# Accumulating transposes for the state-space sums, a reordered Silu, and residuals behind a block border

## The reference

```
x = x + attention(norm(x))      # gated delta rule, 32 value heads of 128
x = x + ffn(norm(x))            # 4-bit weights, 512 -> 1408 -> 512, then y / rms(y)
x = x + state_space(norm(x))    # 512 channels, 16 states
x = x + ffn(norm(x))            # the same weights again
```

```
h[n] = exp(dt * A[n]) * h[n] + dt * x * B[n]
y    = sum over n of h[n] * C[n]          # out = y @ W_out + b
```

## Time and profile before

| | us |
|---|---|
| median of 3 runs | 4491.68 (4491.48 to 4496.43) |
| profiled execution | 4493.62 |
| its span | 4491.8 |
| PE busy | 4303.1 (96%) |
| DVE busy | 3417.9 (76%) |
| ACT busy | 2310.3 (51%) |
| mean granted TensorE clock | 0.986 |

### The profile page before, as it was taken

One profiled execution on the slowest core, in us unless ns is written; L12 is line 12 of the kernel. 1 busy time (PEld: TensorE's weight loads), 2 busy tenths in 40 slices (PEclk: granted clock), 3 DMA queues, 4 the chain that ended last, 5 costly groups with the idle time before them and its releaser, 6 DMA issues. The chain is left out here.

```text
span 4491.8 us, 79320 instructions
## 1 busy us (share of the span) xinstructions
PE 4303.1 (96%) x29557; PEld 2595.2 (58%) x29557; DVE 3417.9 (76%) x8579; ACT 2310.3 (51%) x4841; POOL 433.2 (10%) x342
## 2 busy tenths in 40 slices
PE   7899999999999999999999999998699999999898
PEld 4566666666666666666666666666344444444343
DVE  5888887888877788788788787785446889888950
ACT  4555555555555555555555555554245545554532
POOL 1111111111111111111111111110000000000000
PEclk9999999999999999999999999999899999999999
DMA  2111111101110111110110110100203444444520
GB/s 72 40 37 36 34 36 32 36 32 34 41 32 29 36 36 62 46 32 29 37 36 29 41 32 30 36 29 11 88 1 116 140 134 152 144 154 135 173 73 19
DMA packets 202401, 263.27 MB, mean 59 GB/s; under 512 B 18174, under 2 KB 101378, under 8 KB 202018
## 3 DMA queue, kind: packets, MB, share of 16 engines
q1 hardware_dynamic: 202018, 258.20, 17.9%
HBM read 249.24 MB, written 8.91 MB: 57 GB/s over the span
## 5 line engine op out<-in xcount | busy, mean ns | idle before, releaser
L455 PE MATMUL bank<-xnT,w_qkv 128*128 128x512 f32 x2048 | 928.6, 596 | 4.1 <-ACT raw L741 3.4
L455 PEld LDWEIGHTS bank<-xnT,w_qkv 128*128 128x128 f32 x2048 | 374.7, 192 | 404.6 <-issue 385.9
L1026 DVE SCALAR_TENSOR_TENSOR conv<-raw,conv_w,conv 128x1024 f32<-128x1024 f32 x384 | 495.3, 1290 | 142.4 <-ACT conv L715 133.2
L568 PE MATMUL bank<-w_out_unit,oT 128*128 128x512 f32 x1024 | 504.7, 616 | 7.9 <-ACT oT L781 7.9
L529 PE MATMUL bank<-w_z_unit,xnT 128*128 128x256 f32 x2048 | 487.5, 381 | 0.0
L529 PEld LDWEIGHTS bank<-w_z_unit,xnT 128*128 128x128 f32 x2048 | 371.5, 191 | 41.4 <-issue 1.0
L1237 PE MATMUL bank<-xnT_f,w_gu 128*128 128x512 f32 x704 | 327.6, 609 | 11.1 <-PEq L1560 7.0
L812 ACT ACTIVATE squares<-o 128x128 f32<-128x128 f32 x512 | 153.9, 302 | 336.8 <-DVE o L1070 275.6
L1255 PE MATMUL bank<-w_down,hidden 128*128 128x512 f32 x704 | 316.8, 593 | 1.1 <-DVE x_blocks L1297 1.1
L1245 PE MATMUL bank<-xnT_f,w_gu 128*128 128x512 f32 x704 | 316.5, 592 | 0.0
L655 ACT ACTIVATE q_state<-bank,e_gc 128x128 f32<-128x128 f32 x448 | 140.3, 364 | 263.6 <-PE bank L440 254.8
(11 more groups left out here) (224 smaller groups left out, 7983.6 us busy)
## 6 DMA issues: line engine op xcount, KB each, us to landing
rows_b<-bc_rows SPq DMA_DIRECT2D x256, 256.0 KB, 3.3
rows_c<-bc_rows SPq DMA_DIRECT2D x256, 256.0 KB, 3.4
w_qkv<-in_w_qkv SPq DMA_DIRECT2D x128, 256.0 KB, 2.9
decay<-gc_rows SPq DMA_DIRECT2D x64, 512.0 KB, 3.9
w_z_unit<-in_w_z SPq DMA_DIRECT2D x32, 512.0 KB, 4.4
w_out_unit<-in_w_out SPq DMA_DIRECT2D x32, 512.0 KB, 5.0
x_after<-x SPq DMA_DIRECT2D x16, 256.0 KB, 2.0
x_blocks<-x_after SPq DMA_DIRECT2D x4, 1024.0 KB, 13.2
```

The lines of the kernel that those rows point to most:

```text
L455: made = e.matmul(PROJ[:, :], w_qkv[:, p % 2, j, :], xnT[:, n // HK, j, h * BANK:(h + 1) * BANK], start=j == 0, stop=j == KT - 1)
L568: made = e.matmul(OB[:, :], oT[:, r, :], w_out[:, N % 2, r, :], start=r == 0, stop=r == REP - 1)
L1026: e.scalar_tensor_tensor(acc, raw[:, i % 2, tap:tap + T], conv_w[:, tap, col:col + 1], acc, ALU.mult, ALU.add).then_inc(on["conv"], 1)
```

## The change

There are three edits. In the attention ACT copies raw and u first and applies z's Silu after them; where a unit's z is due, the load of the Exp table follows z's Silu instead of standing before the copies.

In the state space the identity matmul is replaced by four transposes of the pair's sum, 128x128 each, that accumulate in YB, so that YB holds y as [position, channel]. ACT copies it to a new buffer `y_rows`, PE turns that back by channel tile (a new use `y_turn` of the bank WB, at place 0 of the slot 19 after the tile's first step), and ACT copies it to y. Of the out matmuls of stages 0 to 2 the first moves from slot +3 to +4 of the next stage; those of the last stage move from the end of slot +2 to the head of slot +4. Run 7 starts a slot later.

The squares and the residual of run 0 are left out of its block and stand at the head of the next block's ACT and DVE programs.

```diff
-                    if n_z is not None:
-                        N = n_z
-                        e.wait_ge(on["z_evict"], 4 * N + 4)
-                        e.activation(z[:, :, :, :], z[:, :, :, :], ACT.Silu).then_inc(on["z_silu"], 1)
-                    e.preload_act_table_set(EXP_SET)
+                    if n_z is None:
+                        e.preload_act_table_set(EXP_SET)
...
                     e.wait_ge(on["u_pe"], 8 * (n_scan) + t_scan + 1)
                     e.copy(u[:, :, :], two(UB, 0)).then_inc(on["u_copy"], 1)
+
+                if n_z is not None:
+                    e.wait_ge(on["z_evict"], 4 * n_z + 4)
+                    e.activation(z[:, :, :, :], z[:, :, :, :], ACT.Silu).then_inc(on["z_silu"], 1)
+                    e.preload_act_table_set(EXP_SET)
...
-RUN_START = {1: 0, 2: 44, 3: 88, 4: 132, 5: 176, 6: 228, 7: 273}
+RUN_START = {1: 0, 2: 44, 3: 88, 4: 132, 5: 176, 6: 228, 7: 274}
...
+        uses += [(at + 16 * i + 19, 0, ("y_turn", q, i)) for i in range(KT)]
...
-            uses += [(stage_start(q + 1) + (3, 6, 7, 8)[t], 1, ("out", q, t)) for t in range(TILES)]
+            uses += [(stage_start(q + 1) + (4, 6, 7, 8)[t], 1, ("out", q, t)) for t in range(TILES)]
         else:
-            uses += [(stage_start(q + 1) + 2, 1, ("out", q, t)) for t in range(TILES)]
+            uses += [(stage_start(q + 1) + 4, 0, ("out", q, t)) for t in range(TILES)]
...
-                square_down(e, 0)
...
-                add_residual(e, 0)
...
+                elif kind == "y_turn":
+                    e.wait_ge(on["y_copy"], KT * q + i + 1)
+                    made = turn(e, WB, y_rows[:, :])
                 else:
-                    e.wait_ge(on["y_copy"], KT * (q + 1))
+                    e.wait_ge(on["work_read"], WORK_INDEX[("y_turn", q, KT - 1)] + 1)
...
-                    e.matmul(YB[:, :], c["ident"][:, :], drive[:, p % 4, :], start=n == 1, stop=n == NS - 1).then_inc(
-                        on["y_sum"], 1)
+                    for t in range(TILES):
+                        cols = slice(t * P, (t + 1) * P)
+                        made = e.matmul(YB[:, cols], drive[:, p % 4, cols], c["ident"][:, :], start=n == 1 and t == 0,
+                                        stop=n == NS - 1 and t == TILES - 1, is_transpose=True, skip_group_check=True)
+                    made.then_inc(on["y_sum"], 1)
...
+                elif kind == "y_turn":
+                    if i == 0 and q > 0:
+                        e.wait_ge(on["work_made"], WORK_INDEX[("out", q - 1, TILES - 1)] + 1)
+                    e.copy(y[:, i, :], WB[:, :]).then_inc(on["work_read"], 1)
...
+            square_down(e, 0)
             ss_rstd(0)
...
-                    if i == 0 and q > 0:
-                        e.wait_ge(on["work_made"], WORK_INDEX[("out", q - 1, TILES - 1)] + 1)
-                    e.copy(y[:, i, :], YB[:, :]).then_inc(on["y_copy"], 1)
+                    if KT * q + i > 0:
+                        e.wait_ge(on["work_made"], WORK_INDEX[("y_turn", *divmod(KT * q + i - 1, KT))] + 1)
+                    e.copy(y_rows[:, :], YB[:, :]).then_inc(on["y_copy"], 1)
...
+            add_residual(e, 0)
             ss_stats(0)
```

More of the change, by code:

```diff
@@ L1574, in second_half @@
         carry = sb("carry", [P, NS, KT])
-        y = sb("y", [P, KT, BANK])
+        y, y_rows = sb("y", [P, KT, BANK]), sb("y_rows", [P, BANK])
         gate_slot = {at + 4 * i: (R, i) for R, at in RUN_START.items() for i in range(IT)}
```

## The result

The changed kernel takes 4427.71 us (median of four runs, 4426.6 to 4429.21); the kernel before, run beside it, 4494.06 (4491.48 to 4496.78). The ratio is 0.9853, 95% interval 0.9835 to 0.987: 66 us less. The profiled execution of the changed kernel took 4427.73 us, span 4426.0, where the span of before was 4491.8.

What follows compares the result with a forecast made beforehand. PE was taken as the bound, 96% busy, with DVE close behind in the state space; 32.8 + 29 + 1 - 1 = 61.8 us less gave 4430 against the median (chance 0.54), range 4413 to 4448.

Steps and rivals of the forecast that it cites:

- Part 1: Attention: z's Silu behind u's copy on ACT removes PE's whole wait at L552, 31 x 1.06 = 32.8 us; bounds 16, 33.
- Part 2: State space: y sums by transposes take net 46.7 us off PE, of which 29 us come through; bounds 11, 44.
- D: State-space y sums don't run at the short rate, two records a transpose: 20 us lost, 33 gained, 4479; chance 0.04.
- E: State-space y sums: a transpose takes its full 0.273 us; 50 us lost, 33 gained, 4508; chance 0.04.
- The factors three quarters and a half: State space: share of 11.7 us a stage coming through, 8.8 each in stages 0 to 2, 5.9 in stage 3.
- The 2.7 us for a turn behind a turn: State space: four y_turns directly behind a turn ACT must copy out wait 0.68 us each, 2.7 us.
- Rival B: State space: DVE takes over, carry and decay behind y_turn copies; 17 us cost, sums give 12, 4447; chance 0.20.
- Rival C: State space: PE decides throughout, the sums give 44 us, 4415; chance 0.13.
- Rival F: Attention: half of the gain from z's Silu behind u's copy comes back at L568, 4446; chance 0.05.
- Part 3: Border before the state space: run 0's residuals moved; first turn's copy 2.7 us sooner, bc loses 1.7: 1 us gained.
- Part 4: The end, last y sum to out matmuls: y_turn and the wait for y's copy lengthen it, -1 us (0 to -1.5).

Runs made afterwards that it cites:

- run 0: Not a follow-up experiment: a numbered run of work inside the kernel itself, whose squares and residual stood at the end of the preparing block before the change; no time of its own.
- the ordinary matmuls: The changed kernel with the y sums as ordinary f32 matmuls of 128x128 in place of transposes, y_turns still transposes: 4464.06 us, ratio 0.9936 to the kernel before.
- the early Silu: The changed kernel with the Silu of run 1's first gate ahead of the state space's first rstd on ACT: 4432.02 us, ratio 0.9864 to the kernel before.
- part 1 alone: The kernel before with only the attention's order on ACT changed, raw's and u's copies ahead of z's Silu: 4454.86 us, ratio 0.9914.
- part 3 alone: The kernel before with only the squares and residual of run 0 moved into the next block: 4493.0 us, ratio 0.9998.
- parts 2 and 4 alone: The changed kernel with ACT's order in the attention and the border put back as before: 4473.27 us, ratio 0.9955 to the kernel before.
- early Silu with run 6 earlier: The changed kernel with run 1's first Silu ahead of the first rstd and run 6 at slot 224 for 228: 4431.61 us, ratio 0.986 to before.

## Why the prediction was right

It said 4430 and faster; 4427.7 was measured. In the profiled executions, 61.8 less was forecast and 65.9 found (4493.6 and 4427.7). The closeness is in part luck: part 1 was priced 5 us too low and part 2 about 2 too high. By its own steps:

**Part 1, mechanism right, its term 5 us too small.** Forecast 32.8, the upper end of its bounds 33; the attention alone gained 38.0 (start of the last z Silu, 3157.6 to 3119.6). What follows is not late, as argued: PE is without idle time there. But oT's copy is out only 0.15 us before L568 starts, where the prediction's times leave 0.39. Mis-sized was the price of one wait. The profile counts idle time from the modelled end of the instruction ahead, and that end lies late: in the changed kernel L320 is shown until 1474.65, and L552 behind it starts at 1474.49. Taken from start to start it is different. The instruction ahead of L552, in before:

```profile
1490.34 1.13 PE L320 MATMUL bank<-kq 128*128 128x256 f32 x4
```

To L552 at 1492.52 it is 2.18 us; in the changed kernel 0.97 (1473.52 to 1474.49): 1.21 us where the bracket said 1.05. Another 0.11 went behind L552 (L556 came 0.55 us later, now 0.44), most likely the weight load that had nothing to hide behind. That makes 1.32 a unit, close to what the distance of two z Silus shows (95.81 less 94.50). The second slip is the count: the sum took all 31 waits, and two stay, so 29 x 1.32 = 38.3 us, and 38.0 were measured.

**Part 2, size right (27.3 for 29), the share that comes through guessed.** The work came off as computed, 45.2 us for 46.7, 0.44 us for a sum (rivals D and E fell on the first row; the ordinary matmuls show what D would have been, 4464). The 275 ns of the Trainium skill ("TensorE: Matmul & The Clock Gate", Part 4: PE-mode transpose) is not a pitch here: the changed kernel's transposes have 0.109 us each in a group of four.
- The prediction gave two reasons for the share. The first, waits for DVE that a faster PE only reaches sooner, is what the rows show: PE's idle time grew from 28.6 to 43.6 us, nearly all of it beside a busy DVE. The waits that grew, 3.9 us for xn_f, 3.8 for drive, 1.7 for xn_ss and 1.2 for ACT's xnT_f in front of turns, 10.6 of these 15 us, stand where runs and stages meet: normed rows by DVE, a turn, ACT's copy, the next turn. The second, that the two engines are tied step by step so that DVE's idle time can't be moved about, shows only as PE's few waits for drive (four, 10.2 us, for three, 6.4). DVE's total load is not what sets the share: with some 49 us less on it the growth of PE's gaps is the same, 17.8 for 17.9 us. Whether less work of DVE at those borders would let more through stays open.
- The factors three quarters and a half had no measurement behind them. By stage the forecast gains were 8.2, 8.1, 8.1 and 5.9 us, and 6.3, 9.0, 5.1 and 6.9 came. In sum 32.2 of 46.7 was taken as coming through, seven tenths, and 27.3 of 45.2 did, six tenths.
- The 2.7 us for a turn behind a turn: at run 2's turns the wait costs nothing, the hole is there without it. At the three places beside the state space's turns it is real, 1.33, 0.51 and 1.34 us with the turn's own 0.44. How much of that reaches the end is hidden by the clock in the run without turns back.
- By stage 214.5, 228.7, 224.1, 211.9 was forecast, and it became 216.4, 227.8, 227.1 and 210.9. The two that are off by 1.9 and 3.0 us lie under the 4.5 by which the same first stage differs between the full change and the early Silu, so no stage can be called right or wrong.

Rival B (carry behind the copies of turns back) had 0.20 and is refuted: DVE's wait for the carry went from 41.8 to 38.1 us, and taking all turns back out gave 1.3, some 5 at an equal clock. Its sign, stages 0 and 2 unchanged, came in part: they gained least, 6.3 and 5.1. But without turns back these two stages take 219.0 and 226.4 us for 216.4 and 227.1, so B's price of 17 us isn't in them. Rival C (PE alone decides) would have made the stretch 44 us shorter, and it is 27. Rival F didn't come: no wait at L568 outside the attention's end, where both kernels have the same ten.

**Part 3, steps right, its 1 us not told from none.** In the full change 0.7 us went between the attention's last L568 and the first scan (212.0 to 211.3 us), and alone the median is 0.6 less. But with part 1 alone, without this edit, the stretch is 211.7 us too, as with part 3 alone, and the first scan starts at 3373.9 us as in the full change. Both steps show: the first copy comes earlier, and bc gives back a part (5.79 for 5.14). Four turns ahead of it also ran at the lower clock, 1.12 us.

**Part 4, right in the chain**: 0.95 us more between the last sum and the outs, for 1 (its terms, 0.44 + 0.68 - 0.42, give 0.7; the wait for the copy of y was 0.77). It didn't make the end later, since the last sum followed the last scan after 7.29 us for 9.08, so the outs begin 0.8 us sooner after the last scan. Yet the end comes 0.3 us later: 1.1 us are lost behind the outs. There the last of run 7's four turns lasts 1.12 us for 0.65 and its first gate 5.97 for 5.40, at a mean clock of 0.58 (4293.6 to 4301.2 us) where before had 0.74 (4360.4 to 4367.0). The prediction had no term for this.

## What to carry to other kernels

Where one engine is near its limit, price a wait from start to start against the same pair of instructions in a slot without it; the idle time of a view counts from a modelled end and can read a fifth low. For work taken off the bound engine, ask at which places it waits already: there, the gain is a longer wait, and work put there costs little: the turn back among run 2's turns cost nothing, one behind another turn elsewhere up to 1.3 us. Whether the other engine's total load limits the gain is told by making that engine lighter in both kernels and comparing the growth of the gaps. Whether it is the limit at the places of the waits is another question: read there if it has a pause. And set the clock of the two runs side by side before a small difference, or a missing one, is put down to the edit.

## What the runs showed of the hardware

Two things were not expected. First, the same instructions of the same stage took 216.4 us in the full change and 220.9 with the early Silu, and between the scans 879.1 and 884.7 us in the full change and with its parts 2 and 4 alone; in each pair the longer one has the lower granted clock (0.98 for 0.99, 0.97 for 0.98). Over all kernels here the half-clock records lie between some 20 us (ordinary matmuls) and some 38 (early Silu with run 6 earlier). A small edit moves where stretches of lower clock fall, and effects under some 5 us can't be put down to the edit's own mechanism by the time alone; why a stretch falls in one kernel and not in the other stays open. Second, an f32 transpose that adds to a sum in PSUM runs at the rate of one that doesn't, 0.44 us for four, half of the 0.89 of ordinary f32 matmuls of the same shape.
